# A decoder layer on one core: cross-attention heads written out in two halves, maxima transposed in mid-step, projections spread over the steps

## The reference, cut to what matters

```python
x = LN(x + self_attention(x))            # x: 8 x 512 x 256, 16 heads of 16, rotary q and k
x = LN(x + cross_attention(x, ctx))      # q from x, k and v from ctx, with biases
x = LN(x + moe(x))                       # 8 experts, top 2, and a shared one
# attention of one head: softmax(q @ k.T / sqrt(16)) @ v, over 512 keys
```

## Time and profile before

| | |
|---|---|
| median of 3 runs | 1669.99 us (1668.9, 1669.99, 1704.36) |
| the profiled execution: its own time | 1687.87 us |
| its span, first to last instruction | 1686.0 us |
| first and last exp of attention | 58.4 and 1223.6 us |
| self halves with cross tasks | 7, of 69.6 to 74.4 us |
| cross halves between them | 6, of 62.8 to 66.1 us |
| mean granted clock of TensorE | 0.891 |

### The profile page before, as it was taken

One profiled execution on the slowest core, in us unless ns is written; L12 is line 12 of the kernel. 1 busy time (PEld: TensorE's weight loads), 2 busy tenths in 40 slices (PEclk: granted clock), 3 DMA queues, 4 the chain that ended last, 5 costly groups with the idle time before them and its releaser, 6 DMA issues. The chain is left out here.

```text
span 1686.0 us, 27694 instructions
## 1 busy us (share of the span) xinstructions
PE 1458.2 (86%) x8424; PEld 864.6 (51%) x8424; DVE 1116.5 (66%) x2282; ACT 913.2 (54%) x1702; POOL 438.3 (26%) x411
## 2 busy tenths in 40 slices
PE   3977899889989989989998998977858888999994
PEld 2334334434434444443443543333237778999974
DVE  3727578688778877867876887826326644555556
ACT  3351567566656655755665665741715534555544
POOL 4023032023013013102301301001003542666664
PEclk8596899999989988988997998985958879999997
DMA  4214333333333242333333314113033433777662
GB/s 146 82 55 137 102 96 105 120 118 105 104 105 119 65 141 89 89 113 104 107 112 98 115 52 148 46 54 85 1 107 117 160 117 105 135 153 148 124 187 100
DMA packets 110136, 179.85 MB, mean 107 GB/s; under 512 B 20288, under 2 KB 65984, under 8 KB 107968
## 3 DMA queue, kind: packets, MB, share of 16 engines
q1 hardware_dynamic: 95424, 159.11, 29.7%
q0 software_dynamic: 14592, 19.41, 6.4%
HBM read 98.09 MB, written 79.30 MB: 105 GB/s over the span
## 5 line engine op out<-in xcount | busy, mean ns | idle before, releaser
L519 DVE TENSOR_REDUCE nm<-ps_max 128x1 f32<-128x512 f32 x1024 | 640.4, 682 | 164.4 <-PE ps_max L706 155.9
L477 ACT ACTIVATE prob<-ps_sc 128x512 f32<-128x512 f32 x1024 | 556.8, 597 | 323.4 <-PE ps_sc L720 311.9
L706 PE MATMUL ps_max<-qk 48*128 48x512 f32 x1024 | 466.4, 525 | 40.3 <-DVE nm L519 22.7
L720 PE MATMUL ps_sc<-qk 50*128 50x512 f32 x1024 | 432.2, 494 | 71.4 <-ACT prob L477 44.0
L720 PEld LDWEIGHTS ps_sc<-qk 50*128 50x128 f32 x1024 | 178.1, 201 | 414.6 <-ACT prob L477 286.8
L737 PE MATMUL ps_out<-prob,va 128*32 128x512 f32 x2048 | 305.1, 671 | 5.2 <-ACT prob L477 3.4
L706 PEld LDWEIGHTS ps_max<-qk 48*128 48x128 f32 x1024 | 189.3, 207 | 96.0 <-DVE nm L519 72.8
L1471 PE MATMUL ps_gu<-x2f,we 128*128 128x256 f32 (+1 forms) x1344 | 223.4, 321 | 3.2 <-ACT sg L1136 2.4
L1471 PEld LDWEIGHTS ps_gu<-x2f,we 128*128 128x128 f32 x1344 | 189.8, 191 | 21.0 <-ACT sg L1136 2.8
L359 POOL TENSOR_TENSOR rstd<-mv,eps 128x2 f32<-128x2 f32 x32 | 6.4, 202 | 648.3 <-DVE mv L588 648.3
L1471 PE MATMUL ps_dn<-we,hf 128*128 128x256 f32 x864 | 124.8, 301 | 13.8 <-DVE totals L1445 10.1
(11 more groups left out here) (145 smaller groups left out, 1485.9 us busy)
## 6 DMA issues: line engine op xcount, KB each, us to landing
qk<-hbm_self SPq DMA_DIRECT2D x384, 64.0 KB, 2.3
hbm_self<-stage SPq DMA_DIRECT2D x16, 1024.0 KB, 4.2
qk<-hbm_cq SPq DMA_DIRECT2D x192, 64.0 KB, 2.3
qk<-hbm_ck SPq DMA_DIRECT2D x192, 64.0 KB, 2.3
slots_x<-zeros SPq DMA_DIRECT2D x8, 1360.0 KB, 5.9
xs<-slots_x SPq DMA_DIRECT2D x40, 272.0 KB
weraw<-w_moe SPq DMA_DIRECT2D x11, 768.0 KB
hbm_ck<-stage SPq DMA_DIRECT2D x8, 1024.0 KB, 4.4
```

What stands on the lines that cost most here:

```text
L477: nc.scalar.activation(prob[:, s % 2, j, :], ps_sc[:, (HG * s + j) % NSC, :], ACT.Exp, scale=HD ** -0.5).then_inc(exp_done[a], 1)
L519: nc.vector.tensor_reduce(nm[:, g % 2, r:r + 1], ps_max[:, n % NMX, :], axis=AX.X, op=ALU.max, negate=True).then_inc(max_done[a], 1)
L706: nc.tensor.matmul(ps_max[:, n % NMX, :], qk[rows, 0, pair, P * c:P * c + P], qk[rows, 1, pair, :], start=True, stop=True).then_inc(smax_d ...
L720: nc.tensor.matmul(ps_sc[:, n % NSC, :], qk[rows, 1, h // 2, P * c:P * c + P], qk[rows, 0, h // 2, :], start=True, stop=True).then_inc(st_ ...
```

## The change

Three edits in the attention phase.

1. Cross heads go to one array `hbm_cross[m]`, written in two halves by features, as those of self attention are. SP writes m = 0 at step 1 of the self half (after parts 0 of `cq` and `ck`) and m = 1 at step 6, ahead of the `mrows` of the step, where before it wrote both arrays at step 3. A `stack` of cross heads waits for its own m alone. The write of self heads m = 1 moves from step 5 to step 7 of the cross half.
2. The tasks `nm0` and `nm1` move within their step: TensorE transposes at j = 1 (`NM_AT`), ahead of the product with the values, and ScalarE and VectorE split between their j = 1 and j = 2 of the same step, not at the start of the next.
3. The table: `cq` part 0 moves from step 0 of the self half to step 15 of the cross half before, `cq` part 1 from 1 to 2; `q` part 0 from step 0 of the cross half to step 15 of the self half before, and behind it `qf`, `k`, `kf`, `q` part 1 each a step or so earlier; `v` part 1 from 7 to 10; `xt` from 13 and 14 to 12 and 13. The write of `x2` moves from 13 to 14. Engines that do a step's tasks one step later now carry those of step 15 into the next half (`former`).

```diff
 TASKS = {
     FIRST: {
-        0: [("cq", 0, -1), ("ck", 0, -1)], 1: [("nm0", 1, 0), ("ot1", 0, -2), ("cq", 1, -1)], 2: [("ot1", 1, -2)],
-        3: [("ot1", 2, -2), ("ck", 1, -1)], 4: [("ot1", 3, -2), ("cv", 0, -1)], 5: [("nm0", 2, 0), ("cv", 1, -1)],
...
+        0: [("ck", 0, -1)], 1: [("nm0", 1, 0), ("ot1", 0, -2)], 2: [("ot1", 1, -2), ("cq", 1, -1)],
+        3: [("ot1", 2, -2), ("ck", 1, -1)], 4: [("ot1", 3, -2), ("cv", 0, -1)], 5: [("nm0", 2, 0), ("cv", 1, -1)], 7: [("nt1", 0, -2)],
...
+        12: [("ln1", 0, -2)], 13: [("nm1", 0, -1), ("x1b", 0, -1)], 15: [("q", 0, 1)],
     SECOND: {
-        0: [("q", 0, 1)], 1: [("nm1", 1, -1), ("ot0", 0, 0), ("k", 0, 1), ("qf", 0, 1)], 2: [("ot0", 1, 0)],
-        3: [("kf", 0, 1), ("ot0", 2, 0), ("q", 1, 1)], 4: [("k", 1, 1), ("qf", 1, 1), ("ot0", 3, 0)],
-        5: [("nm1", 2, -1), ("kf", 1, 1), ("v", 0, 1)], 6: [("nt0", 0, 0)], 7: [("nt0", 1, 0), ("v", 1, 1)],
-        8: [("w0", 0, 0)], 9: [("nm1", 3, -1), ("w0", 1, 0)], 11: [("ln0", 0, 0)], 12: [("c", 0, 0)],
-        13: [("nm0", 0, 1), ("xt", 0, 0)], 14: [("xt", 1, 0)],
+        0: [("qf", 0, 1), ("k", 0, 1)], 1: [("nm1", 1, -1), ("ot0", 0, 0)], 2: [("kf", 0, 1), ("ot0", 1, 0), ("q", 1, 1)],
+        3: [("ot0", 2, 0), ("k", 1, 1)], 4: [("qf", 1, 1), ("ot0", 3, 0)], 5: [("nm1", 2, -1), ("kf", 1, 1), ("v", 0, 1)],
+        6: [("nt0", 0, 0)], 7: [("nt0", 1, 0)], 8: [("w0", 0, 0)], 9: [("nm1", 3, -1), ("w0", 1, 0)], 10: [("v", 1, 1)],
+        11: [("ln0", 0, 0)], 12: [("xt", 0, 0), ("c", 0, 0)], 13: [("nm0", 0, 1), ("xt", 1, 0)], 15: [("cq", 0, 0)],
...
+        def former(half, s, k):
+
+            if s:
+                return tasks(half, s - 1, k)
+            return tasks(FIRST, STEPS - 1, k) if half == SECOND else tasks(SECOND, STEPS - 1, k - 1)
...
-                    sp.wait_ge(ck_out, out_c)
-                    sp.wait_ge(cq_out, out_c)
+                sp.wait_ge((cross_out if a else self_out)[m], b * 16 + 16)
...
+                    if h == FIRST and s in (1, 6) and exists(k - 1):
+                        m = s // 6
+                        sp.wait_ge(lo_done["cq"], upto("cq", k - 1, m))
+                        sp.wait_ge(lo_done["ck"], upto("ck", k - 1, m))
+                        sp.dma_start(hbm_cross[m], stage[:, m, :, :].bitcast(F32)).then_inc(cross_out[m], 16)
...
-                    if h == FIRST and s == 3 and exists(k - 1):
-                        sp.wait_ge(lo_done["ck"], upto("ck", k - 1, 1))
-                        sp.dma_start(hbm_ck, stage[:, :, 2:4, :].bitcast(F32)).then_inc(ck_out, 16)
-                        sp.wait_ge(lo_done["cq"], upto("cq", k - 1, 1))
-                        sp.dma_start(hbm_cq, stage[:, :, 0:2, :].bitcast(F32)).then_inc(cq_out, 16)
-                    if h == SECOND and s in (3, 5) and exists(k + 1):
+                    if h == SECOND and s in (3, 7) and exists(k + 1):
...
-                    if h == FIRST and s == 13 and exists(k - 2):
+                    if h == FIRST and s == 14 and exists(k - 2):
...
@@ (ScalarE; VectorE's half() changes alike) @@
-                    for kind, n, b in tasks(h, s - 1, k):
-                        task(kind, n, b, cur, prv)
+                    for kind, n, b in former(h, s, k):
+                        if kind not in ("nm0", "nm1"):
+                            task(kind, n, b)
                     for j in range(HG):
+                        if j == NM_AT + 1:
+                            for kind, n, b in tasks(h, s, k):
+                                if kind in ("nm0", "nm1"):
+                                    rows_hi(kind, n, b, cur, prv)
...
@@ (TensorE) @@
-                        if j == JOB_AT:
-                            for kind, n, b in tasks(h, s, k):
-                                if kind in job_done:
-                                    job(kind, n, b, k)
+                        for kind, n, b in tasks(h, s, k):
+                            if kind in job_done and j == (NM_AT if kind in ("nm0", "nm1") else JOB_AT):
+                                job(kind, n, b, k)
```

More of the change, by code:

```diff
@@ L23 @@
 PV_AT = 2
+NM_AT = 1
 JOB_AT = 3
@@ L80, in wait_alone, with attention_phase @@
     eng.wait_ge(s, value)
-def attention_phase(nc, x, xT, cT, w_att, tables, b_cols, bo_rows, x2, hbm_self, hbm_ck, hbm_cq, slots_x, sums):
+def attention_phase(nc, x, xT, cT, w_att, tables, b_cols, bo_rows, x2, hbm_self, hbm_cross, slots_x, sums):
     with ExitStack() as ctx:
@@ L143, in attention_phase @@
         self_out = [sem(f"self_out{m}") for m in range(FC)]
-        ck_out, cq_out = sem("ck_out"), sem("cq_out")
+        cross_out = [sem(f"cross_out{m}") for m in range(FC)]
         stack_in = [[sem(f"stack_in{a}{g}") for g in range(NG)] for a in range(2)]
@@ L250, in stack @@
                     for s, part in ((0, qp), (1, kp)):
[L251 to L254, removed]
+                        src = (hbm_cross if a else hbm_self)[m, rows, 2 * s + part, :]
                         for par in range(2):
@@ L290, in half @@
                             mrows(int(kind[2]), b, n)
-                    if h == FIRST and s == 3 and exists(k - 1):
-                        sp.wait_ge(lo_done["ck"], upto("ck", k - 1, 1))
-                        sp.dma_start(hbm_ck, stage[:, :, 2:4, :].bitcast(F32)).then_inc(ck_out, 16)
-                        sp.wait_ge(lo_done["cq"], upto("cq", k - 1, 1))
-                        sp.dma_start(hbm_cq, stage[:, :, 0:2, :].bitcast(F32)).then_inc(cq_out, 16)
-                    if h == SECOND and s in (3, 5) and exists(k + 1):
-                        m = (s - 3) // 2
+                    if h == SECOND and s in (3, 7) and exists(k + 1):
+                        m = s // 7
                         sp.wait_ge(lo_done["k"], upto("k", k + 1, m))
@@ L404, in head_outputs, with task @@
                 nc.scalar.activation(ot[:, g, :], ps_out[:, :], ACT.Copy).then_inc(oev_done[a], 1)
-            def task(kind, n, b, cur, prv):
+            def task(kind, n, b):
                 if kind in ("qf", "kf"):
                     act.wait_ge(roped[kind[0]], upto(kind[0], b, n))
[L409 to L412, removed]
+                    if exists(b - 2):
+                        act.wait_ge(cross_out[n], (b - 2) * 16 + 16)
                     c = 0 if kind == "qf" else 1
@@ L446, in task, with rows_hi @@
                     split_hi(kind, b, n, xf[:, HI, n, :], bank(kind, n))
[L447 to L456, removed]
+            def rows_hi(kind, n, b, cur, prv):
+                if n >= 2:
+                    mrow_wait((int(kind[2]), b), n - 2)
+                elif n == 1 and prv:
+                    mrow_wait(prv, 3)
+                elif n == 0 and (cur or prv):
+                    mrow_wait(cur or prv, 2)
+                split_hi(kind, b, n, mst[:, n % 2, HI, :], bank(kind, n)[0:HG * TT, 0:P])
             def half(h, k):
@@ L603, in half @@
                     turn = maxima_of(s, cur, nxt)
-                    for kind, n, b in tasks(h, s - 1, k):
-                        task(kind, n, b)
+                    for kind, n, b in former(h, s, k):
+                        if kind not in ("nm0", "nm1"):
+                            task(kind, n, b)
                     for j in range(HG):
+                        if j == NM_AT + 1:
+                            for kind, n, b in tasks(h, s, k):
+                                if kind in ("nm0", "nm1"):
+                                    task(kind, n, b)
                         if turn:
@@ L1615, in _ @@
             down(NJ - 1)
-SCRATCH = {"x2": [TOKENS + CAP, D], "hbm_self": [FC, P, SLOTS, T], "hbm_ck": [P, FC, 2, T], "hbm_cq": [P, FC, 2, T],
+SCRATCH = {"x2": [TOKENS + CAP, D], "hbm_self": [FC, P, SLOTS, T], "hbm_cross": [FC, P, SLOTS, T],
            "slots_x": [CHUNKS, P, CT, ROW], "sums": [TOKENS + CAP, D]}
@@ L1623, in program @@
     attention_phase(nc, ap["x"], ap["xT"], ap["cT"], ap["w_att"], ap["tables"], ap["b_cols"], ap["bo_rows"],
-                    scratch["x2"], scratch["hbm_self"], scratch["hbm_ck"], scratch["hbm_cq"], scratch["slots_x"],
+                    scratch["x2"], scratch["hbm_self"], scratch["hbm_cross"], scratch["slots_x"],
                     scratch["sums"])
```

5 lines of the change are left out of this document (removed), and 3 rows, old and new, of the table TASKS.

## The result

The changed kernel takes a median of 1599.2 us in 4 runs (1593.9 to 1609.8), the kernel before 1677.8 in the same session: a ratio of 0.956, 95% interval [0.946, 0.965]. The forecast, 1605 against 1670, is a ratio of 0.961. The profiled execution took 1609.8 us with a span of 1608.1; before, the span was 1686.0, so 77.9 us of span went, at a mean granted clock of 0.915 in place of 0.891.

A forecast was written before the change was run, and what follows sets the result against it. Cross halves were taken as nearly full of matmul work, self halves as losing time to TensorE's waits and half clock. Terms summed to -65 us, 1670 to 1605; own bounds 1592 to 1620, range with rivals 1576 to 1638.

The forecast's parts named there:

- Wait and clock, steps 7 to 9, -48: Seven self halves: scores no longer wait for late maxima, nor half clock follow: 48 us less, within 39 and 57.
- the rival in which it stays: Self halves: the wait goes but half clock stays, only 25 of 48 us gained: 1628, or up to 1656; chance 0.18.
- The gap, -11: Self half after the last self attention, without scores: restacking and maxima start earlier, 11 us less, within 8 and 13.
- Steps 0 to 2 of the self half, -17: Moved projections and no bank wait at step 1: 14.37 us becomes 11.9, 17 us less over seven halves.
- `q` and `cq` at step 15, +5, +2, +3 for half clock: Projections added at step 15: `q` costs 5 us in self halves, `cq` 2 in cross halves, half clock 3 more.
- Cross halves, -1 within 6: Six cross halves: moved tasks' gains and costs nearly cancel, 1 us less, within 6 each way; step 1 about 4.1.
- The start, 0 within 2: Cross half at the beginning, without scores: `q` part 0 leaves the gap, `cq` part 0 enters: 0, within 2 us.
- Maxima in mid-step, +2 within 0 and 18: 64 steps: the 0.28 us transposing matmul now stands where TensorE waits for nothing: 2 us more, within 0 and 18.
- the rival's size (96 us): Mid-step transposition waits for VectorE's reductions, 1.5 us in each of 64 steps, 96 us: 1701; chance 0.04.
- The late half clock stays: Steps 14, 15 and 0, four of seven self halves: no change expected; rival that it goes, 1583, chance 0.15.
- the cause that I took: Late half clock of self halves: follows a TensorE idle of 1.18 us, in which the maxima wait for VectorE's norm.

The follow-up runs named there:

- e1: Kernel before with only the cross heads written in two halves, at steps 1 and 6 of the self half: ratio 0.964 to the kernel before, 60 us less.
- e4: Changed kernel with the cross heads' writes in two halves undone: ratio 0.978 to the kernel before, 38 us more than the changed kernel.
- e7: Changed kernel with GpSimd's task `x1b` moved from step 13 of the self half to step 6 of the cross half: ratio 0.951 to the kernel before.
- e8: Changed kernel with periods 2 to 6 written out instead of looped over: ratio 0.954 to the kernel before.
- e2: Kernel before with only the maxima transposed and split in mid-step: ratio 0.993 to the kernel before, 12 us less.
- e6: Changed kernel with the old task table: ratio 0.960 to the kernel before, 7.5 us more than the changed kernel.
- e5: Changed kernel with the maxima back at j = 3 and split one step later: ratio 0.962 to the kernel before, median 1613.7 us.
- e3: Kernel before with only the new task table and its moved writes of self heads and `x2`: ratio 0.989 to the kernel before, 18 us less.
- e9: Changed kernel with `k` ahead of `qf` at step 0 of the cross half: ratio 0.951 to the kernel before.
- e10: Changed kernel with `k` ahead of `qf` at step 0 and `v` part 1 back at step 7 of the cross half: ratio 0.947 to the kernel before.
- e11: Changed kernel with the changes of e7 and e10 together: ratio 0.948 to the kernel before.
- e12: Kernel of e11 with periods 2 to 6 written out as well: ratio 0.936 to the kernel before, median 1551.4 us.

## Why the prediction was right, and where it was off

The time was right (forecast ratio 0.961, measured 0.956, forecast within the interval), and so was the mechanism: the late rows of maxima and the half clock behind them. Self halves of about 66 and cross halves of 65 us were forecast, and came out at 64.0 and 62.5 in the mean. By its own steps:

- **Wait and clock, steps 7 to 9, -48.** Measured -42.6, within the bounds of 39 and 57. The steps take 3.47, 3.64 and 4.47 now, 11.6 together, where I had read 10.1 from other halves; that is the miss. e1 shows that edit 1 does it alone, e4 that the other two edits don't. The half clock went with the wait in every one of the seven halves; the rival in which it stays falls. The rule of the Trainium skill named there ("TensorE: Matmul & The Clock Gate", section "A second HAM failure mode: psum-queue depth-cycling") is borne out in part: no new fall came in the steady cross halves, whose clock is 1.00 though their steps got thinner, but in e7 and e8 falls appeared in places that had held none in the changed kernel.
- **The gap, -11.** Measured -11.6; the first maximum 11.0 earlier. Right, with e1 (47.6) as its proof.
- **Steps 0 to 2 of the self half, -17.** Measured -20.1. Five of the halves lost 2.2 to 2.3, as taken with 2.5; the other two lost 5.0 and 3.8, because in the kernel before their step 0 was at half clock (8.13 and 6.97 us). e2 shows that the earlier read alone takes 1.15 off the 5.81 of step 1, where I had read a wait of 0.83.
- **`q` and `cq` at step 15, +5, +2, +3 for half clock.** Self +2.9, cross +6.1. Without half clock `q` adds 0.65 to a self step (3.60 to 4.25), as taken; only three of seven had half clock there (6.46, 6.21 and 5.04), before it was four. `cq` adds 1.0 to a cross step where 0.3 was taken: 3.3 to 4.4 in the two halves without a turn of the loop, 4.9 to 5.9 in the four with one. I had counted on the turn to hide it, and it hides nothing.
- **Cross halves, -1 within 6.** Measured -13.4, +6.1 of step 15 included, so -19.6 for what this term priced. This step failed, and by the most. I said that VectorE would set step 1 at about 4.1. It took 3.08 in all six (6 us), and step 4 lost 1.4 where I had taken 0.5 (5 us). Steps 10 to 14 got 1.15 longer where 1.9 was taken (4.5 us). And step 0 lost 4.0 in sum: in four of the halves before, the late half clock had run on into it (5.4 to 5.5 us in place of 3.9), now in none. The window of a step 1:

```profile
747.00:750.08 3.08, 3.08 (x21) 1.52 (x21) 3.08 (x8) 2.30 (x6) 2.83 (x3) 1.00 0.56 182
```

VectorE is busy for all of it, but with work that reaches over both borders: the first read of `k` begins at 746.46, ahead of the step, and two of the four reductions end at 750.38, behind it; `ps_max` has three buffers. Over steps 0 to 4 it is busy for 19.2 of 20.2 us, and TensorE for 20.1. So what an engine must do in a step doesn't set the length of that step; only a sum over several does. The table's part in the cross halves is 7.4 us with edit 2 there (e6), 14.2 without it (e1 389.9, e5 375.7): edits 2 and 3 both take the bank wait out of step 1, so their gains don't add.
- **The start, 0 within 2.** It cost +3.5 and the first half with its gap +6.2. This was missed. The 3.5 are the table's: the first exp comes at 61.4 to 62.6 us in the six kernels with the new table and `k` and `v` as in it, and at 57.6 to 58.4 in the four with the old one. The 6.2 are its in part only: that stretch takes 103.6 to 112.5 with the new table (e3 left out), 105.6 to 108.0 with the old, by where the half clock lies in it; the last step with the gap takes 55.5 to 60.8 against 52.6 to 56.2. The timeline of the start, before and then after:

```profile
26.45 2.49 POOL L334 TENSOR_TENSOR stage<-cosq,stage 128x512 fp32r<-128x512 f32 x2
...
29.04 0.33 SPq L299 DMA_DIRECT2D hbm_self<-stage  x1
```
```profile
24.49 1.26 POOL L331 TENSOR_TENSOR stage<-cosq,stage 128x512 fp32r<-128x512 f32 x1 [0.74 <-ACT stage L386]
25.71 1.27 POOL L340 TENSOR_TENSOR res<-res,trig 128x512 f32<-128x512 f32 x1
...
30.44 0.33 SPq L296 DMA_DIRECT2D hbm_self<-stage  x1
...
46.31 2.93 PE L629 MATMUL ps_job<-w,xf 128*128 128x256 f32 x12
...
49.99 0.69 DVE L519 TENSOR_REDUCE nm<-ps_max 128x1 f32<-128x512 f32 x1 [2.67 <-PE ps_max L711]
```

GpSimd now splits `q` before it rotates `k`, and with no scores to hide it `k` is on the path: the first write comes 1.4 us later, and with it the first maximum (41.62 against 40.23). e9 gives that back (1.5 us). And `v` part 1 at step 10 now stands among the maxima, which begin at step 9, at half clock: 2.93 us in which VectorE idles for 2.67. With `v` back in e10 the first exp comes 2.9 earlier than in e9, and the last step with the gap falls from 56.5 to 52.1. In that gap `cq` part 0 now stands ahead of the first score as well, at half clock, for 2.9 us (170.62 to 173.48), where I had taken 0; no run moves it alone. I had asked of the moved projections what they do in steady halves and at the gap's start, not what they now stand ahead of.
- **Maxima in mid-step, +2 within 0 and 18.** e5 puts it at 0 in the profiled span, and 11 us to the good by ratios whose intervals overlap. Whether it gains anything in the changed kernel stays open; a cost of the rival's size (96 us) is ruled out.
- **The late half clock stays.** It did at steps 14 and 15 in 3 of 7 (before 4 of 7), and e7, e11 and e12 bear out the cause that I took: with the norm short it came in none of the 15 halves where the norm had been long. The one in the last self half begins ahead of the norm; its cause stays open. What the prediction didn't foresee is the half clock at other places.

The sum of the misses: +5 at steps 7 to 9, -3 at steps 0 to 2, -5 at step 15 of the self halves, -14 in the cross halves with their step 15, +10 at the start and in the first half, -2 for the maxima, +2 in the last half, -5 in the MoE phase, whose code is the same. They cancel to within 13 us of the profiled time (1623 forecast, 1609.8 measured), so that the total is better than its terms. For the median luck helped once more: I took 17.9 us off the profiled time, and here the median lies 10.6 below it, which brings 1605 within 6 us of 1599.2.

## What to carry to other kernels

When one transfer is late, look at what stands ahead of it in its queue: the rows of maxima were ready 5.9 us before they left, and halving the write that `stack` waited for was worth five times what making the rows ready earlier was (60 us in e1, 12 in e2). Sum an engine's load over as many steps as its buffers let it lag, not step by step. And price a moved task at the program's ends too, where nothing hides it.

## What the runs showed of the hardware

- Four `tensor_scalar` of VectorE (128x256) took 1.37 us alone (e7) and 2.74 beside four `tensor_tensor` of GpSimd, while GpSimd's four took 2.96 in place of 2.80. The Trainium skill ("SBUF — State Buffer", section "Who interferes with whom") says that the two contend for a shared pair of ports when VectorE is in a two-port mode, which `tensor_scalar` can enter, that the one that issues first holds the pair for its whole instruction, and that the other fully blocks. The trace agrees: each of VectorE's four records ends 0.15 us behind one of GpSimd's (at 731.03, 731.78, 732.51 and 733.25, against 730.88, 731.63, 732.36 and 733.10), one for one. The records overlap all the same, so the time of a record here seems to hold the waiting too. In which mode VectorE ran, no run shows.
- A turn of the engines' loop cost 1.45 us of a step (e8), and about as much in the kernel before (4.9 against 3.3).
- The half clock turned up in other places from kernel to kernel: at step 0 behind the loop turn (e7, e11), at steps 9, 14 and 15 (e8), and nowhere in the stretch of e12 that is shown. One fall costs 1.3 us (a step 0 of 5.60 in e7 where 4.3 is its full-clock time) to 4.7 (as worked out ahead), so an edit that removes one us of idle can be worth 5, or nothing.
